# Second attention, blocks of 256 keys: VectorE writes only the negated maximum, ScalarE exponentiates straight from the score bank

## Chip, cores and metric

The kernel runs on one core of one Trainium2 chip. The metric is device microseconds of one execution. TensorE (PE) multiplies, VectorE (DVE), ScalarE (ACT) and GpSimd (POOL) work on its results, SyncE (SP) issues most transfers. PSUM is the accumulator that PE writes and that DVE and ACT read.

## What is computed

Two gated layers over 8 sequences of 256 tokens, width 128. Layer 1 is a recurrence beside a two-deep local-attention network; layer 2 is the attention that this change touches, gated by a mixture of 16 experts (two per token). The part that matters:

```python
def _L1_attn_ref(x, Wq, Wk, Wv, Wo, bo):      # B 2 (here 8 sequences), S 256, 16 heads of 8
    q = (x @ Wq.T).reshape(b, s, H, DK).transpose(0, 2, 1, 3)
    ...
    scores = jnp.einsum('bhqd,bhkd->bhqk', q, k)
    scores = jnp.where(causal, scores, -jnp.inf)
    attn = jax.nn.softmax(scores / np.sqrt(DK), axis=-1)
    ctx = jnp.einsum('bhqk,bhkd->bhqd', attn, v)
    ...
    return ctx @ Wo.T + bo
```

## The kernel before

The 16 token tiles are handled in four turns of four tiles. The program is a chain of sections: HEAD, FIRST (turn 0), BODY (a loop that runs twice), TAIL, LAST, and then the experts. The second attention of a turn runs in the section after it, so it stands in BODY (twice), TAIL and LAST. A planner (`section_order`) writes the order of items for each engine from a table of costs, `PARTS`, and engines work strictly in that order; the items of the other network are interleaved with it.

For each sequence `b` (0, 1) of a turn the second attention has three blocks `q`. Block 0 is the first 128 queries against 128 keys, four heads to a bank; blocks 1 and 2 are the last 128 queries against all 256 keys, two heads to a bank. A block has two pairs `h` of two units; a unit is one PSUM bank of 128x512 scores. The items of a pair are written here as in the planner:

- `bS b q h` on PE (`score_rows`): two mask matmuls, one into each of the two score banks `psS0`, `psS1`, then the scores. The next `bS` or `S` (a pair of the first attention, `scores`) writes the same two banks.
- `bS b q h` on DVE (`less_maxima_of_pair`, L1420 and L1426): per unit a maximum for each head into `MX`, then scores less maximum into the SBUF buffer `PR` (four units deep). The subtraction releases the bank (`s_free`).
- `bE b q r` on ACT (`exponentials`): one Exp of 128x512 in place in `PR`, then `exp_done`.
- `bT b q r` on PE turns the probabilities into the banks `psT`, ACT copies them out (`keep_probs`); `bP` sums with the values, `bN` on DVE normalises.

So PE waits for DVE alone before it writes the score banks again, and ACT may take the Exp much later. Around the change stand these items too: `wo` and `sh` (output product and token shift of the first attention), `w1`, `w2` (its feed-forward part; Gelu on ACT), `qk`, `scale` (DVE and POOL work on queries and keys), `x` (a turn of the activations), `w13`, `w2t` (in LAST: turning expert weights).

Of the kernel before, what the change touches and what calls it, by code (L numbers as in the profile page):

```python
# [18 lines left out]
ALU = mybir.AluOpType  # L19
ACT = mybir.ActivationFunctionType  # L20
AX = mybir.AxisListType.X

P = 128
# [381 lines left out]
class Section:  # L405
# [25 lines left out]
    def turned_before(self, n):  # L431

        return [self.T[unit_item("T", u)] for u in self.S if self.S[u] == n] or self.earlier("T")

    def earlier(self, name):

        n = self.before.get(name, 0)
        return [n - 2, n - 1]
# [38 lines left out]
WIDE = 2 * FE + 2 * D  # L477

T_A0 = T_P_USES // 2
D_FIRST_STEPS, D_A_STEPS, P_A_STEPS = 48, 76, 24  # L480


D_HEAD_STEPS, P_HEAD_STEPS = 1, 5
# [2 lines left out]
def gated_layers(nc, ins, out):  # L486
    ctx = ExitStack()
    with ctx:
# [6 lines left out]
        def pair(name):  # L495
# [3 lines left out]
        Tb, Mb, Sb, Ob = ([ctx.enter_context(nc.psum_tensor(f"ps{n}{i}", [P, 512], F32)) for i in range(2)]  # L499
                          for n in "TMSO")  # L500
        t_full, t_free = pair("t_full"), pair("t_free")
        m_full, m_free = pair("m_full"), pair("m_free")
        s_full, s_free = pair("s_full"), pair("s_free")
        o_free = pair("o_free")
        exp_done = pair("exp_done")
# [25 lines left out]
        PR = sb("PR", [P, 4, 512])  # L531
        PT = sb("PT", [P, 2, 512])
        MX = sb("MX", [P, 4, 4])
# [305 lines left out]
        def _(pe):  # L839
# [12 lines left out]
                    pe.wait_ge(m_free.sem(e), m_free.did(hm, e))  # L852
                return Mb[n % 2]

            def scores(b, qt, hs, n):


                for i in range(2):
                    pe.wait_ge(s_free.sem(n + i), s_free.reuse(hs, n + i))
                    pe.sem_inc(pe_settled, 1)  # L860
                    r = slice(64 * i, 64 * i + 64)
                    for w in range(2):
                        nc.tensor.matmul(Sb[i][64 * w:64 * w + 64, :], identb[r, r],
                                         ((mask0[0], mask1)[qt] if w == i else swapped[qt])[r, :], start=True, stop=False,
                                         skip_group_check=True)
                for c in range(4):
                    for w in range(2):
                        for i in range(2):
                            r = slice(64 * i, 64 * i + 64)
                            q = b * SEQ + qt * P + 64 * w  # L870
                            keys = own_keys(2 * qt + w, r, c, b)
                            o = Sb[i][64 * w:64 * w + 64, c * P:(c + 1) * P]
                            if 2 * qt + w == 2:
                                o = o.rearrange("p (w k) -> p w k", w=2)
                            last = nc.tensor.matmul(o, QT[r, c, q:q + 64], keys, start=False, stop=c == 3,  # L875
                                                    skip_group_check=True)
                            if c == 3 and w == 1:
                                last.then_inc(s_full.sem(n + i), 1)
# [17 lines left out]
                    last = mm(bank[64:P, o], p[:, 64:P], VA[:, 2 * b + qt, head, :])  # L896
                last.then_inc(pv_done.sem(o_use), 1)

            def score_rows(b, q, h, hs, n):


                qt, keys = int(q > 0), P * (1 + (q > 0))
                for i in range(2):
                    pe.wait_ge(s_free.sem(n + i), s_free.reuse(hs, n + i))
                    nc.tensor.matmul(Sb[i][:].rearrange("p (i k) -> p i k", k=keys)[:, :, qt * P:keys], identb[:],
                                     mask0[1][:, 0:512 // (qt + 1)].rearrange("p (i k) -> p i k", k=P),
                                     start=True, stop=False, skip_group_check=True)
                for c, lane in enumerate((range(4), (0, 1), (2, 3))[q]):
                    for i in range(2):
                        r = slice(NS * (2 * h + i), NS * (2 * h + i) + NS)  # L910
                        last = nc.tensor.matmul(Sb[i][:, c * keys:(c + 1) * keys], QL[r, b, lane, qt * P:(qt + 1) * P],  # L911
                                                KT1[r, b * SEQ:b * SEQ + keys], start=False,
                                                stop=(c + 1) * keys == 512, skip_group_check=True)
                        if (c + 1) * keys == 512:
                            last.then_inc(s_full.sem(n + i), 1)
# [30 lines left out]
            def run(sec, it, ahead):  # L946
                ht, hm = T_A0 + uses_before(sec, it, "T"), uses_before(sec, it, "M")
                hs, hq, ho = uses_before(sec, it, "S"), uses_before(sec, it, "QK"), uses_before(sec, it, "O")
# [6 lines left out]
                for item in sec.order["PE"]:  # L955
                    kind, *of = item
                    if kind == "x":
                        l, b = of
# [5 lines left out]
                        for t in range(2):  # L964
                            last = nc.tensor.transpose(bank[:, t * P:(t + 1) * P], XC[:, 2 * b + t, :], ident[:])  # L965
                        last.then_inc(t_full.sem(sec.T[item]), 1)
                    if kind == "ab":
                        copied(("x", 0, 1), earlier=True)
                        bank = m_open(hm, sec.M[item])
                        for i in range(2):  # L970
                            for b in range(2):
                                last = mm(bank[NS * b:NS * b + NS, i * SEQ:(i + 1) * SEQ], WABC[:, i, :],
                                          XNT[:, b * SEQ:(b + 1) * SEQ])
                        last.then_inc(m_full.sem(sec.M[item]), 1)
                    if kind == "c":
                        bank = m_open(hm, sec.M[item])
                        for b in range(2):
                            last = mm(bank[NS * b:NS * b + NS, 0:SEQ], WABC[:, 2, :], XNT[:, b * SEQ:(b + 1) * SEQ])
                        last.then_inc(m_full.sem(sec.M[item]), 1)
                    if kind == "y":  # L980
                        pe.wait_ge(cs_done, it + 1)
                        bank = m_open(hm, sec.M[item])
                        for t in range(GT):
                            mm(bank[:, t * P:(t + 1) * P], CS[0:2 * NS, (t % 2) * P:(t % 2 + 1) * P],
                               WYP[0:2 * NS, t // 2, :], True, False)
                            last = mm(bank[:, t * P:(t + 1) * P], XNT[:, t * P:(t + 1) * P], WD, False, True)
                        last.then_inc(m_full.sem(sec.M[item]), 1)
                    if kind in ("qk", "v"):
                        l, n = of
# [7 lines left out]
                    if kind == "qkT":  # L997
                        l, n = of
# [7 lines left out]
                    if kind == "S":  # L1006
                        l, b, qt = of
                        if sec is FIRST:
                            pe.wait_ge(ld_masks, 16 * 4)
                        if sec is FIRST and (l, b, qt) == (0, 0, 0):  # L1010
                            pe.wait_ge(pool_consts, POOL_CONSTS)
                        if qt == 0:
                            if (l, b) == (0, 0):
                                copied(earlier=True)
                            else:
                                copied(("qkT", l, 4 * b + 2), ("qkT", l, 4 * b + 3))
                        scores(b, qt, hs, sec.S[l, b, 2 * qt])
                    if kind == "T":
                        turn_probs(ht, sec.T[item], hs, sec.S[*of])
                    if kind == "V":  # L1020
# [4 lines left out]
                    if kind == "oT":  # L1025
                        l, t = of
# [80 lines left out]
                    if kind == "bS":  # L1107
                        b, q, h = of
                        if q == h == 0:
                            pe.wait_ge(q_masked, it * 8 + 4 * b)  # L1110
                        score_rows(b, q, h, hs, sec.S["b", b, q, 2 * h])
                    if kind == "bT":
                        turn_probs(ht, sec.T[item], hs, sec.S["b", *of])
                    if kind == "bP":
# [91 lines left out]
        def _(act):  # L1206
# [6 lines left out]
            def exponentials(hs, n):  # L1213
                act.wait_ge(s_free.sem(n), s_free.did(hs, n))
                act_fn(PR[:, n % 4, :], PR[:, n % 4, :], ACT.Exp).then_inc(exp_done.sem(n), 1)
# [12 lines left out]
            def run(sec, it, ahead):  # L1228
# [13 lines left out]
                for item in sec.order["ACT"]:  # L1242
# [77 lines left out]
                    if kind == "bqk":  # L1320
# [3 lines left out]
                        act.wait_ge(q_masked, it * 8 + (4 * b - 4))  # L1324
                        act_fn(QRAW[:], bank[:, 0:SEQ], ACT.Copy, scale=DK1 ** -0.5)
                        act_fn(KT1[:, b * SEQ:(b + 1) * SEQ], bank[:, SEQ:2 * SEQ], ACT.Copy).then_inc(free, 1)
                    if kind == "bE":
                        exponentials(hs, sec.S["b", *of])
                    if kind == "bT":
                        b, q, r = of  # L1330
                        n = B_UNITS * b + 4 * q + r
                        before = sec.earlier("O") if n < 8 else [sec.O["bP", (n - 8) // B_UNITS, int((n - 8) % B_UNITS > 3)]]
                        keep_probs(ht, sec.T[item], ho, before, PTB[:, n % 8, :])
# [61 lines left out]
        def _(dve):  # L1395
# [17 lines left out]
            def less_maxima_of_pair(hs, n, turned, ht, ns):  # L1413

                before = steps[1]
                scores = [Sb[i][:].rearrange("p (s k) -> p s k", s=ns) for i in range(2)]
                maxima = [MX[:, (n + i) % 4, 0:ns] for i in range(2)]
                for i in range(2):
                    dve.wait_ge(s_full.sem(n + i), s_full.did(hs, n + i))
                    V.tensor_reduce(maxima[i], scores[i], AX, ALU.max).then_inc(dstep, 1)  # L1420
                    steps[1] += 1
                for i in range(2):
                    dve.wait_ge(dstep, steps[0] + before + i + 1)
                    for u in turned[i]:
                        dve.wait_ge(t_full.sem(u), t_full.did(ht, u))
                    V.tensor_tensor(PR[:, (n + i) % 4, :].rearrange("p (s k) -> p s k", s=ns), scores[i],  # L1426
                                    maxima[i].unsqueeze(2).broadcast_to([P, ns, 512 // ns]), ALU.subtract)\
                        .then_inc(s_free.sem(n + i), 1)
# [40 lines left out]
            def run(sec, it, ahead):  # L1469
# [22 lines left out]
                for item in sec.order["DVE"]:  # L1492
# [133 lines left out]
                    if kind == "bS":  # L1626
                        b, q, h = of
                        n = sec.S["b", b, q, 2 * h]
                        less_maxima_of_pair(hs, n, [sec.turned_before(n + i - 4) for i in range(2)], ht, 2 if q else 4)
                    if kind == "bN":  # L1630
                        b, qt = of
                        o = sec.O["bP", b, qt]
# [371 lines left out]
```

## Time and profile before

| | us |
|---|---|
| median of 3 runs | 886.46 (882.73 to 886.53) |
| span of the profiled execution | 918.4 |
| BODY, its second pass, about | 174 |
| VectorE busy | 642.1 |
| ScalarE busy | 496.9 |
| PE busy (matmuls) | 708.3 |

The profile is of one execution; its own time, first to last instruction, is the span of 918.4 us, and no other time of that execution is given. It lies 31.9 us above the median of the timed runs. Busy time is the time an engine had an instruction at work; where it waited, the views name the engine and line whose end released it.

### The profile page before, as it was taken

To read this page: it belongs to the slowest core of one execution; us is meant where nothing else is said; L and a number is where in the kernel's file an instruction comes from. 1 tells how busy PE (TensorE), PEld (TensorE's weight loads), DVE (VectorE), ACT (ScalarE), POOL (GpSimd) and SP (SyncE) were. 2 spreads that over 40 slices of the span, in tenths; PEclk is the share of its full clock that TensorE was granted. 3 is DMA by queue.
4 is the path that set the end of the run, shared out by engine and by line. 5 is a ranking of instruction groups with operands and counts; after the bars stand their busy time and mean duration, and the time that the engine had idled before them with its cause. 6 is when DMAs were issued, how large, how long until landed. Compare 5 with 4: busy or idle time off the path is not lost.

```text
span 918.4 us, 20712 instructions
## 1 busy us (share of the span) xinstructions
PE 708.3 (77%) x7336; PEld 530.8 (58%) x7351; DVE 642.1 (70%) x1521; ACT 496.9 (54%) x893; POOL 392.0 (43%) x470
## 2 busy tenths in 40 slices
PE   4688887689899867998997798999859309798830
PEld 1456554457676734676675466658646207698830
DVE  5586776697869775977986797787658325476645
ACT  2444555465666753656676566655726205487711
POOL 7351633560714063434412760480041750068880
PEclk9789999899999997999999999999978759799975
DMA  8600000000000000000000000000023313122104
GB/s 206 177 1 1 1 1 1 1 1 3 1 2 1 2 1 3 2 1 2 1 2 1 1 1 2 1 2 2 1 87 87 119 42 128 36 70 70 62 35 146
DMA packets 43839, 30.03 MB, mean 33 GB/s; under 512 B 7650, under 2 KB 41692, under 8 KB 43484
## 3 DMA queue, kind: packets, MB, share of 16 engines
q1 hardware_dynamic: 39932, 23.17, 8.7%
q0 software_dynamic: 2560, 5.25, 1.5%
q8 instruction: 64, 1.05, 0.5%
q10 hardware_dynamic: 1248, 0.28, 0.2%
q14 instruction: 35, 0.29, 0.1%
HBM read 18.98 MB, written 9.44 MB: 31 GB/s over the span
## 4 chain that ended last, share of the span: by engine, by line
PE 38%; DVE 24%; issue 13%; POOL 13%; ACT 6%; another core or an unknown queue 4%; DMA 1%; DVEq 1%; POOLq 0%; ACTq 0%; SPq 0%
PE psM L841 14%; DVE arena L1538 5%; PE psO L926 4%; ACT arena L1208 4%; DVE PR L1426 4%; PE psT L884 4%; POOL yt_scratch L1918 3%; PE psS L875 3%; PE psS L911 3%; POOL arena L1895 3%; POOL arena L1892 3%; POOL RS L1871 2%; DVE MX L1420 2%; DVE arena L1546 2%
## 5 line engine op out<-in xcount | busy, mean ns | idle before, releaser
L841 PE MATMUL psM<-arena 128*128 128x128 f32 (+7 forms) x1168 | 267.9, 372 | 44.1 <-DVE arena L1538 25.3
L1208 ACT ACTIVATE arena<-psT 128x512 f32<-128x512 f32 (+2 forms) x296 | 150.8, 530 | 153.9 <-PE psT L1003 37.1
L841 PEld LDWEIGHTS psM<-arena 128*128 128x128 f32 (+5 forms) x1168 | 155.5, 190 | 93.0 <-DVE arena L1538 38.1
L1208 ACT ACTIVATE arena<-psM 128x512 f32<-128x512 f32 (+2 forms) x168 | 88.3, 543 | 114.3 <-PE psM L841 113.3
L1420 DVE TENSOR_REDUCE MX<-psS 128x4 f32<-128x512 f32 (+1 forms) x160 | 102.7, 682 | 62.5 <-issue 24.0
L1870 POOL TENSOR_SCALAR RS<-MV 128x2 f32<-128x2 f32 x56 | 14.4, 256 | 293.2 <-DVE MV L1574 167.5
L1892 POOL TENSOR_TENSOR arena<-arena,powm 128x8 f32<-128x8 f32 x64 | 109.9, 1717 | 5.3
L1208 ACT ACTIVATE PR<-PR 128x512 f32<-128x512 f32 x160 | 94.6, 626 | 21.1 <-DVE PR L1426 20.9
L1426 DVE TENSOR_TENSOR PR<-psS,MX 128x512 f32<-128x512 f32 x160 | 102.1, 678 | 0.0
L884 PE MATMUL psT<-ident,PR 128*128 128x128 f32 x640 | 94.3, 282 | 5.4 <-ACT PR L1208 1.9
L884 PEld LDWEIGHTS psT<-ident,PR 128*128 128x128 f32 x640 | 74.9, 145 | 34.1 <-issue 27.0
L1895 POOL TENSOR_TENSOR arena<-arena 128x512 f32<-128x512 f32 x64 | 85.7, 1339 | 0.0
L1538 DVE TENSOR_TENSOR arena<-psM,arena 128x512 f32<-128x512 f32 x128 | 81.7, 679 | 0.0
L1208 ACT ACTIVATE arena<-arena 128x768 f32 (+3 forms) x61 | 46.6, 763 | 49.9 <-DVE arena L1806 30.0
L1546 DVE TENSOR_TENSOR arena<-arena 128x512 f32<-128x512 f32 x64 | 55.1, 878 | 15.3 <-POOL arena L1895 15.2
L1891 POOL TENSOR_SCALAR arena<-arena 128x8 f32<-128x8 f32 x64 | 17.9, 280 | 104.6 <-DVE arena L1525 104.3
L1208 ACT ACT_TABLE_LOAD x43 | 55.2, 1283 | 10.0 <-PE psT L965 9.3
L1525 DVE TENSOR_REDUCE arena<-arena 128x8 f32<-128x512 f32 x64 | 43.4, 678 | 21.0 <-ACT arena L1208 20.6
L1003 PE MATMUL psT<-ident,arena 128*128 128x128 f32 x256 | 40.8, 287 | 19.9 <-DVE arena L1546 19.8
L911 PE MATMUL psS<-arena 32*128 32x256 f32 (+1 forms) x512 | 55.7, 346 | 0.0
L1918 POOL DMA_INDIRECT yt_scratch<-arena,DEST x48 | 49.7, 1036 | 12.1 <-issue 7.3
L1906 POOL TENSOR_SCALAR arena<-arena,lanem 128x256 f32<-128x256 f32 x32 | 29.2, 934 | 55.8 <-ACT arena L1208 55.8
(198 smaller groups left out, 1163.8 us busy)
## 6 DMA issues: line engine op xcount, KB each, us to landing
arena<-in_L_ffn_w SPq DMA_DIRECT2D x50, 128.0 KB
xg_scratch<-zeros SPq DMA_DIRECT2D x12, 256.0 KB, 3.7
arena<-xg_scratch SPq DMA_DIRECT2D x12, 256.0 KB
arena<-yt_scratch SPq DMA_DIRECT2D x4, 512.0 KB, 5.3
arena<-in_L_ffn_wqkv SPq DMA_DIRECT2D x2, 768.0 KB, 5.0
arena<-in_L_ffn_ln_g SPq DMA_DIRECT2D x1, 1024.0 KB, 5.3
arena<-in_L_ffn_ln_b SPq DMA_DIRECT2D x1, 1024.0 KB, 8.5
out<-arena SPq DMA_DIRECT2D x4, 256.0 KB, 2.2
```

What stands on the lines that cost most here:

```text
L841: return nc.tensor.matmul(o, lhsT, rhs, start=start, stop=stop)
L884: last = nc.tensor.transpose(bank[:, c * P:(c + 1) * P], PR[:, m % 4, c * P:(c + 1) * P], ident[:])
L911: last = nc.tensor.matmul(Sb[i][:, c * keys:(c + 1) * keys], QL[r, b, lane, qt * P:(qt + 1) * P], KT1[r, b * SEQ:b * SEQ + keys], start=False,
L1208: return nc.scalar.activation(o, i, f, **kw)
L1420: V.tensor_reduce(maxima[i], scores[i], AX, ALU.max).then_inc(dstep, 1)
L1426: V.tensor_tensor(PR[:, (n + i) % 4, :].rearrange("p (s k) -> p s k", s=ns), scores[i], maxima[i].unsqueeze(2).broadcast_to([P, ns, 512 // ...
L1525: V.tensor_reduce(SS[:, m % 4, :], SQ[:, m % 2, :].rearrange("p (h d) -> p h d", h=8), AX, ALU.add).then_inc(ss_done.sem(m), 1)
L1538: last = V.tensor_tensor(dst.rearrange("p (h d) -> p h d", h=8), src, RT[:, 2 * l + n % 2, x, t % 2, :].unsqueeze(1) .broadcast_to([P, 8, ...
L1546: V.tensor_tensor(r1, r1, RN[:, m % 4, :].unsqueeze(2).broadcast_to([P, 8, DH]), ALU.mult)\
L1892: G.tensor_tensor(RN[:, m % 4, :], RN[:, m % 4, :], powm[:, 0:8], ALU.pow)
L1895: G.tensor_tensor(r1, r1, r2[:, :, ::-1, :], ALU.add).then_inc(rope_sum.sem(m), 1)
L1918: G.indirect_dma_start(YT, bass.IndirectOffsetOnAxis(DEST[:, tile:tile + 1], 0), YO[:, tile % OUT_RING, :], None)\
```

## The change

For the blocks with 256 keys (`q` 1 and 2) DVE no longer subtracts: it takes the maximum with the sign turned and releases its claim on the bank. ACT reads the bank itself: two Exp of 128x256 a unit, with the head's negated maximum as the bias. PE, before it writes a bank whose last unit was of this kind, now also waits for that unit's `exp_done`. The constant 76 counted DVE steps of a BODY and becomes 60. The planner's costs stay, so no item moves.

```diff
+    def read_by_exponent(self, n):
+
+        unit = next((u for u in self.S if self.S[u] == n), None)
+        return unit is None or (unit[0] == "b" and unit[2] > 0)
...
-D_FIRST_STEPS, D_A_STEPS, P_A_STEPS = 48, 76, 24
+D_FIRST_STEPS, D_A_STEPS, P_A_STEPS = 48, 60, 24
...
-            def scores(b, qt, hs, n):
+            def scores(sec, b, qt, hs, n):
...
                 for i in range(2):
                     pe.wait_ge(s_free.sem(n + i), s_free.reuse(hs, n + i))
+                    if sec.read_by_exponent(n + i - 2):
+                        pe.wait_ge(exp_done.sem(n + i), exp_done.reuse(hs, n + i))
...
-                    if kind == "bE":
+                    if kind == "bE" and of[1] == 0:
                         exponentials(hs, sec.S["b", *of])
+                    if kind == "bE" and of[1]:
+                        n = sec.S["b", *of]
+                        act.wait_ge(s_free.sem(n), s_free.did(hs, n))
+                        for u in sec.turned_before(n - 4):
+                            act.wait_ge(t_full.sem(u), t_full.did(ht, u))
+                        for i in range(2):
+                            keys = slice(i * 2 * P, (i + 1) * 2 * P)
+                            last = act_fn(PR[:, n % 4, keys], Sb[n % 2][:, keys], ACT.Exp, bias=MX[:, n % 4, i:i + 1])
+                        last.then_inc(exp_done.sem(n), 1)
...
-                        less_maxima_of_pair(hs, n, [sec.turned_before(n + i - 4) for i in range(2)], ht, 2 if q else 4)
+                        if q == 0:
+                            less_maxima_of_pair(hs, n, [sec.turned_before(n + i - 4) for i in range(2)], ht, 4)
+                        for i in range(2 if q else 0):
+                            dve.wait_ge(s_full.sem(n + i), s_full.did(hs, n + i))
+                            V.tensor_reduce(MX[:, (n + i) % 4, 0:2], Sb[i][:].rearrange("p (s k) -> p s k", s=2),
+                                            AX, ALU.max, negate=True).then_inc(s_free.sem(n + i), 1)
```

The same two waits are added in `score_rows`. How it stands on the engines, in BODY, at the pair `bS 0 1 1` and the pair after it, `bS 0 2 0`:

On DVE, behind the last Gelu product of `w1 0 0 2`, `bS 0 1 1` was this (L1420 the maxima, L1426 the subtractions, L1595 and L1598 the item `w2 0 0`):

```order
L1588 SCALAR_TENSOR_TENSOR arena<-psM,arena 85x256
L1419 REGISTER_ALU
L1420 TENSOR_REDUCE MX<-psS 128x2 x2
L1425 REGISTER_ALU
L1426 TENSOR_TENSOR PR<-psS,MX 128x512
L1423 REGISTER_ALU
L1425 REGISTER_ALU
L1426 TENSOR_TENSOR PR<-psS,MX 128x512
L1478 REGISTER_ALU
L1595 TENSOR_TENSOR arena<-arena,psM 128x256
```

Now it is this:

```order
L1606 SCALAR_TENSOR_TENSOR arena<-psM,arena 85x256
L1650 REGISTER_ALU
L1651 TENSOR_REDUCE MX<-psS 128x2 x2
L1496 REGISTER_ALU
L1613 TENSOR_TENSOR arena<-arena,psM 128x256
```

The two subtractions are gone and `w2` follows the maxima at once. On ACT, the Exp of that pair (`bE 0 1 2`, `bE 0 1 3`) stood behind two copies of `oT` and a table load:

```order
L1208 ACTIVATE arena<-psT 128x512
L1208 ACTIVATE arena<-psM 128x512
L1208 ACTIVATE arena<-psT 128x512
L1214 REGISTER_ALU
L1208 ACT_TABLE_LOAD
L1208 ACTIVATE PR<-PR 128x512 x2
L1239 REGISTER_ALU
```

They stand at the same place now, four in number, and read the bank:

```order
L1217 ACTIVATE arena<-psT 128x512
L1217 ACTIVATE arena<-psM 128x512
L1217 ACTIVATE arena<-psT 128x512
L1340 REGISTER_ALU
L1217 ACT_TABLE_LOAD
L1217 ACTIVATE PR<-psS,MX 128x256 x4
L1248 REGISTER_ALU
```

Nothing moved in the order; the source and the number of the Exp changed. On PE, `bS 0 2 0` follows the turn `oT 0 1` and stands ahead of `wo 0 1`, `qk 1 2` and the turns of the probabilities of `bS 0 1 1` (in brackets the semaphores that an instruction waits for):

```order
L1032 MATMUL psT<-ident,arena 128x128 [waits t_free1,o_free0]
L1032 MATMUL psT<-ident,arena 128x128 x3
L904 REGISTER_ALU
L905 MATMUL psS<-maskc,identb 128x2x128 [waits s_free0]
L905 MATMUL psS<-maskc,identb 128x2x128 [waits s_free1]
L911 MATMUL psS<-arena 128x256 x4
L953 REGISTER_ALU
L852 REGISTER_ALU [waits t_free1,t_free0]
L841 MATMUL psM<-arena 128x128 [waits m_free0]
```

Now the same rows wait for the Exp of the pair before as well:

```order
L1041 MATMUL psT<-ident,arena 128x128 [waits t_free1,o_free0]
L1041 MATMUL psT<-ident,arena 128x128 x3
L911 REGISTER_ALU
L914 MATMUL psS<-maskc,identb 128x2x128 [waits exp_done0,s_free0]
L914 MATMUL psS<-maskc,identb 128x2x128 [waits exp_done1,s_free1]
L920 MATMUL psS<-arena 128x256 x4
L962 REGISTER_ALU
L857 REGISTER_ALU [waits t_free1,t_free0]
L846 MATMUL psM<-arena 128x128 [waits m_free0]
```

Only the waits changed; everything behind the mask matmuls on PE is behind those waits.

## Rows read from the trace of the kernel before

**Rows 1.** The page: its span, and the chain that ended last, by engine and line

```profile
span 918.4 us, 20712 instructions
...
PE 38%; DVE 24%; issue 13%; POOL 13%; ACT 6%; another core or an unknown queue 4%; DMA 1%; DVEq 1%; POOLq 0%; ACTq 0%; SPq 0%
PE psM L841 14%; DVE arena L1538 5%; PE psO L926 4%; ACT arena L1208 4%; DVE PR L1426 4%; PE psT L884 4%; POOL yt_scratch L1918 3%; PE psS L875 3%; PE psS L911 3%; POOL arena L1895 3%; POOL arena L1892 3%; POOL RS L1871 2%; DVE MX L1420 2%; DVE arena L1546 2%
```

**Rows 2.** Busy time by engine, second BODY (stretch; length, PE, PEld, DVE, ACT, POOL)

```profile
346.00:520.00 174.00, 147.75 (x1650) 107.36 (x1650) 135.65 (x288) 106.17 (x184) 68.41 (x74) 0.97 0.01 2
```

**Rows 3.** Groups by line and form: count, busy us, mean ns, idle before

```profile
L1426 DVE TENSOR_TENSOR PR<-psS,MX 128x512 f32<-128x512 f32 x160 | 102.1, 678 | 0.0
L1420 DVE TENSOR_REDUCE MX<-psS 128x2 f32<-128x512 f32 x64 | 41.0, 682 | 10.2 <-PE psS L911 10.1
L1208 ACT ACTIVATE PR<-PR 128x512 f32<-128x512 f32 x160 | 94.6, 626 | 21.1 <-DVE PR L1426 20.9
L1208 ACT ACTIVATE arena<-psM,arena 128x256 f32<-128x256 f32 x32 | 14.4, 473 | 9.2 <-PE psM L841 9.0
```

**Rows 4.** Timeline, BODY, around `bS 0 1 0` and `S 0 1 0`: start, length

```profile
385.51 1.27 PE L875 MATMUL psS<-arena 64*64 64x128 f32 x32
385.89 1.15 ACT L1208 ACTIVATE PR<-PR 128x512 f32<-128x512 f32 x2
387.74 1.95 PE L926 MATMUL psO<-arena 128*32 128x128 f32 x64
389.63 0.40 PE L863 MATMUL psS<-maskl,identb 64*64 64x512 bf16 x1
```

**Rows 5.** Timeline, BODY, from `bS 0 1 1` on: start, length, idle before

```profile
402.40 1.28 DVE L1426 TENSOR_TENSOR PR<-psS,MX 128x512 f32<-128x512 f32 x2
404.52 0.44 PE L965 MATMUL psT<-ident,arena 128*128 128x128 f32 x2 [0.52 <-DVE arena L1598]
409.44 0.38 PE L905 MATMUL psS<-maskc,identb 128*128 128x256 bf16 x2
410.30 1.28 ACT L1208 ACT_TABLE_LOAD   x1
410.81 2.91 PE L841 MATMUL psM<-arena 128*128 128x128 f32 x18
411.60 1.15 ACT L1208 ACTIVATE PR<-PR 128x512 f32<-128x512 f32 x2
414.29 0.41 DVE L1561 TENSOR_TENSOR arena<-arena,psM 128x256 f32<-128x256 f32 x1
427.47 0.69 DVE L1546 TENSOR_TENSOR arena<-arena 128x512 f32<-128x512 f32 x1 [2.26 <-POOL arena L1895]
```

**Rows 6.** Timeline, TAIL, behind `bS 0 1 1` and behind `bS 0 2 1`

```profile
568.87 0.84 ACT L1208 ACTIVATE arena<-psM,arena 128x256 f32<-128x256 f32 x2
570.18 0.28 PE L905 MATMUL psS<-maskc,identb 128*128 128x256 bf16 x1 [1.98 <-DVE PR L1426]
571.02 1.15 ACT L1208 ACTIVATE PR<-PR 128x512 f32<-128x512 f32 x2
575.76 0.42 DVE L1561 TENSOR_TENSOR arena<-arena,psM 128x256 f32<-128x256 f32 x1 [1.13 <-PE psM L841]
...
588.42 0.38 PE L905 MATMUL psS<-maskc,identb 128*128 128x512 bf16 x1
589.02 1.15 ACT L1208 ACTIVATE PR<-PR 128x512 f32<-128x512 f32 x2
```

**Rows 7.** Timeline, LAST: a long wait on ACT, and the last pairs

```profile
755.19 0.60 ACT L1208 ACTIVATE arena<-psT 128x512 f32<-128x512 f32 x1 [32.01 <-remote]
...
779.59 0.27 PE L905 MATMUL psS<-maskc,identb 128*128 128x256 bf16 x1
780.07 1.14 ACT L1208 ACTIVATE PR<-PR 128x512 f32<-128x512 f32 x2
784.65 0.66 PE L884 MATMUL psT<-ident,PR 128*128 128x128 f32 x4 [0.99 <-ACT PR L1208]
```

More of the change, by code:

```diff
@@ L897, in values, with score_rows @@
                 last.then_inc(pv_done.sem(o_use), 1)
-            def score_rows(b, q, h, hs, n):
+            def score_rows(sec, b, q, h, hs, n):
                 qt, keys = int(q > 0), P * (1 + (q > 0))
@@ L904, in score_rows @@
                     pe.wait_ge(s_free.sem(n + i), s_free.reuse(hs, n + i))
+                    if sec.read_by_exponent(n + i - 2):
+                        pe.wait_ge(exp_done.sem(n + i), exp_done.reuse(hs, n + i))
                     nc.tensor.matmul(Sb[i][:].rearrange("p (i k) -> p i k", k=keys)[:, :, qt * P:keys], identb[:],
@@ L1016, in run @@
                                 copied(("qkT", l, 4 * b + 2), ("qkT", l, 4 * b + 3))
-                        scores(b, qt, hs, sec.S[l, b, 2 * qt])
+                        scores(sec, b, qt, hs, sec.S[l, b, 2 * qt])
                     if kind == "T":
@@ L1110, in run @@
                             pe.wait_ge(q_masked, it * 8 + 4 * b)
-                        score_rows(b, q, h, hs, sec.S["b", b, q, 2 * h])
+                        score_rows(sec, b, q, h, hs, sec.S["b", b, q, 2 * h])
                     if kind == "bT":
```

## The prediction

> **What bounds the kernel now.** I read the page's chain first, then the busy times of one BODY, then the timelines around the pairs that change. The chain passes through PE for 38%, DVE for 24%, POOL for 13%, and through no single engine for long [rows 1]. In the second BODY, of 174 us PE is busy 147.75, DVE 135.65, ACT 106.17, POOL 68.41 [rows 2]: PE is the fullest, DVE close behind, ACT has the most room of the engines that change. The chain hops between them, so what a pair is worth is decided at its own place: whoever comes last there. The reader should see that DVE is at times the last (the subtractions L1426 are 4% of the chain), and that ACT, although it is seldom the last, takes some Exp very late: the pair `bS 0 1 1` is subtracted at 402.40 and exponentiated at 411.60 [rows 5]. Before, nobody minded: the score banks were free since the subtraction. That is the state the change touches.
>
> **What is removed.** 64 subtractions at 678 ns (32 pairs: 8 in each BODY, 8 in TAIL, 8 in LAST) leave DVE. Two of them take 1.28 us as a pair, and the next instruction starts about 1.2 us after the first [rows 3, 5], so 38 us of DVE time go in all, 9.6 in a BODY. The maxima stay; I take the negated ones at the old 682 ns [rows 3].
>
> **What is added on ACT.** Two Exp of 128x512 took 1.15 us together, a start every 0.53 [rows 5]. Four of 128x256 with a bias pointer come instead, from PSUM. The trace has that shape as the Gelu of `psM` with a bias: 473 ns alone [rows 3], two in 0.84, so a start every 0.37 [rows 6]. A pair then takes 3 x 0.37 + 0.47 = 1.6 us, 0.45 more; 32 pairs make 14 us on ACT. The first bank is released about 0.85 us after the first Exp starts, the second after 1.6. Bounds: if starts came every 0.30 a pair would take 1.4, if they didn't overlap, 4 x 0.47 = 1.9. [...]
>
> **What is added on PE: a wait.** A `bS` or `S` behind a changed pair now waits until that pair's Exp have read both banks. The first mask matmul waits for the first bank, the second for the second, and the scores stand behind both; behind them stands everything else on PE. Three places show the sizes.
>
> BODY, `bS 0 1 0`: Exp starts at 385.89, behind copies that the change doesn't touch, so the banks are free at 386.75 and 387.5. PE wrote the scores of `S 0 1 0` at 385.51 [rows 4]: 2.0 us later now. Behind them stand turns and a `bP` that kept PE busy right up to 389.63, when the next `S` began; `y` and `w1` follow on a full PE. DVE would have been 1.2 us early there, but has to wait for these scores. I charge 1.9.
>
> BODY, `bS 0 1 1`: PE is ready at 409.44. ACT is at a copy, then the table load at 410.30, then the Exp at 411.60 [rows 5]; none of that depends on DVE, so it stays. The second bank is free at 413.2: PE stands for 3.7 us, with `wo 0 1`, `qk 1 2`, the turns and `sh` behind it. `wo` is 16 of the 18 matmuls of 2.91 us that follow the scores, so its result comes 2 us after them, and DVE's L1561 goes from 414.29 to 416.7, 2.4 late although it had 1.2 us in hand. The next pair's missing subtractions give back 1.2; the rest, 1.2, goes into POOL's chain for `scale`, for which DVE waits at 427.47 [rows 5], and on to PE. Charge 1.2. Ahead of it stands a gain: the turn `x 1 0` at 404.52 waited 0.52 for DVE behind the subtractions of 402.40 [rows 5]: minus 0.5. The later four pairs of a BODY find ACT prompt and either PE or POOL last; I take them at zero, between minus 0.5 and plus 0.5.
>
> One BODY: 1.9 + 1.2 - 0.5 = 2.6, two make 5.2.
>
> TAIL: PE, which wrote at 570.18 after waiting for DVE, gets the banks from Exp that start at 571.02: 571.9 and 572.6. That is 1.9 late, and the path behind it is PE's: DVE waited for `wo` at 575.76. Charge 1.9. At 588.42 PE would have to wait for the Exp of 589.02, so until 590.6, 2.2 late with two `qk` items of the POOL chain behind it: 2.2 [rows 6]. In the second sequence two more waits of this kind, together some 4.5 us on PE, meet a stretch where the missing subtractions give most of it back; I charge 1.2. Together 5.3.
>
> LAST: one wait of 2.2 comes early and puts all that follows back, the routing too. ACT then stands 32.01 us until 755.19 [rows 7] for something that no engine of the program released; a further delay ahead of it may vanish there. Of the last pairs ACT is the busiest engine: PE wrote at 779.59, the Exp ran at 780.07, so the banks come at 781.7 at the best, and PE and ACT, each behind the other twice, end some 3.0 late where PE waits for ACT at 784.65 [rows 7]. Charge 5.2.
>
> **Sum.** 5.2 + 5.3 + 5.2 = 15.7 us. I take off 2 us for places where freed DVE time (38 us) helps that I didn't find: 13.7. Against the profiled execution that is 918.4 to about 932; the timed median lies 31.9 us below that span, near the size of the one long wait on ACT, which may belong to the profiled execution only. I add the difference to the median: 886.5 + 13.7, so about **900 us**, 1.5% slower. A difference of 0.5%, 4.4 us, is about what a measurement of this kernel can tell from none.
>
> **Rivals.**
>
> *DVE's relief wins* (16%): faster. If DVE is last more often than I read, the missing subtractions shorten the chain. L1426 is 4% of the chain, 36 us for 160 of them; 64 of those are 14.7 us. If the waits cost only half of what I charge (7.9), the kernel gains 6.8: 880. At its best, with waits hidden, 872. It decides if PE's 3.7 us in BODY are absorbed before L1561: then each BODY is at least 1 us ahead. For it speaks that DVE is busy 78% of a BODY and that Exp of a prompt pair can start up to 1.2 us earlier; against it, that at the places above ACT's start is fixed by copies and table loads.
>
> *The two cancel* (14%): within 4.4 us of before, 882 to 891, about 888. For it speaks the spread: eleven or so pairs gain, ten lose, and a kernel in which four engines are interleaved absorbs a late microsecond often.
>
> *The waits add up* (9%): nothing is absorbed. Raw PE waits are about 5.9 in a BODY, 8.7 in TAIL, 7 in LAST: 27.5 together, 914. It would need PE to have no idle time behind each wait; it has 26 us in a BODY [rows 2], so I hold this unlikely.
>
> *My forecast* (61%): some of each wait reaches the end; its own range is 892 to 910.
>
> **Range and chances.** Faster 0.16, same 0.14, slower 0.70 (forecast and adding up). The range 882 to 912 leaves out most of the faster case and the end of the adding-up one, about 2 in 10; the price of the Exp (1.4 to 1.9 a pair, over some ten waits plus or minus 3 us) lies within it.
>
> **What would show it.** DVE busy about 43 us less, ACT 14 to 16 more. In BODY, PE idle some 3.7 us ahead of the mask matmul of `bS 0 2 0`, released by ACT's Exp; a BODY of 176.6 instead of 174; PE idle of about 2 us released by ACT at five or so more mask matmuls. Wrong would be: the Exp of `bS 0 1 1` starting earlier than right behind its table load; Exp of 128x256 far from 0.47; a BODY shorter than 174, which would mean that DVE's relief is on the path; or the long wait of LAST moving, which no step here covers.

## The result and the profile after

The changed kernel takes 917.38 us (median of 4, 916.08 to 920.84) against 886.5 (882.73 to 888.35) in the runs beside it, where 900 was forecast and 912 was the upper end. The medians are 3.5% apart; the ratio of the runs is 1.0376 [1.0329, 1.0423] (in brackets, here and below, the 95% interval). One timed run below, the 919.47 of `e8_short_fill`, counts as a slow one and is left out of its ratio. The direction was right; the loss is 31 us instead of 13.7.

The execution profiled of before was an unusual one: its wait of 32.01 us on ACT in LAST [rows 7] is in no other profile here, and its span of 918.4 less this wait gives 886.4, close to the timed median. In the executions of the changed kernel the span is 2 us below the time. So no two spans are subtracted below; the stages are compared, each from its first score mask matmul on PE to that of the next (LAST in two pieces around the long wait: to the mask matmul of its seventh pair, and from the Exp of the eighth to the end of the last pair's Exp):

| us | BODY 1 | BODY 2 | TAIL | LAST, first | LAST, then |
|---|---|---|---|---|---|
| before | 173.4 | 170.0 | 169.7 | 29.7 | 18.0 |
| changed | 177.9 | 177.0 | 175.2 | 36.9 | 23.2 |
| `e1_wait_alone` | 177.7 | 174.1 | 174.7 | 36.2 | 20.4 |
| `e2_relief_alone` | 170.2 | 166.4 | 166.9 | 28.9 | 17.6 |
| `e3_filled_wait` | 177.9 | 176.7 | 175.3 | 36.9 | 23.2 |
| `e5_prompt_pairs` | 172.7 | 169.4 | 170.5 | 29.0 | 18.4 |
| `e6_late_pairs` | 177.3 | 177.3 | 174.7 | 37.0 | 22.8 |
| `e7_one_exp` | 176.6 | 174.5 | 174.8 | 36.2 | 21.8 |
| `e8_short_fill` | 174.5 | 173.0 | 178.5 | 36.7 | 23.2 |
| `e11_body_moved` | 172.4 | 174.8 | 178.8 | 36.7 | 23.2 |
| `e9_moved` | 172.9 | 171.1 | 171.6 | 35.7 | 21.6 |
| `e10_moved_before` | 176.8 | 175.5 | 171.0 | 34.8 | 21.9 |
| `e12_placed` | 170.8 | 169.7 | 169.0 | 29.1 | 18.0 |
| `e13_placed_last_direct` | 172.4 | 171.3 | 169.0 | 36.5 | 21.3 |

The changed kernel loses 4.5 and 7.0 in the BODYs, 5.5 in TAIL, 7.2 and 5.2 in LAST: 29.4. Each row is one execution, and a pass of the same code differs by a microsecond or two from one kernel to the next (the BODYs of the last two rows, by 1.6), which is the grain of this table. The table also shows that a BODY of before is 173.4 or 170.0, not the 174 from which the prediction gave 176.6.

The page of the changed kernel, the chain by engine (answers to [rows 1]):

```profile
PE 42%; DVE 18%; POOL 14%; issue 13%; ACT 11%; DMA 1%; DVEq 1%; POOLq 0%; ACTq 0%; SPq 0%
```

Groups by line and form (to [rows 3]):

```profile
L1217 ACT ACTIVATE PR<-psS,MX 128x256 f32<-128x256 f32 x128 | 50.1, 480 | 3.4 <-DVE MX L1651 3.3
L1651 DVE TENSOR_REDUCE MX<-psS 128x2 f32<-128x512 f32 x64 | 41.1, 683 | 39.5 <-PE psS L920 39.4
```

PE's largest waits (engine, what it waits for: total, times, longest):

```profile
PE psS L914 <- ACT PR L1217: 23.6, 22, 3.8
PE psM L846 <- DVE arena L1556: 21.4, 24, 2.0
```

DVE has become lighter, 601.7 us busy instead of 642.1, and went from 24% of the chain to 18%; ACT went from 6% to 11%. The largest wait of PE is one that did not exist before: the mask matmul behind the Exp. ACT is busy for 508.6 us instead of 496.9, 11.7 more where 14 to 16 were forecast. VectorE now stands 39.4 us ahead of the maxima of these pairs, where it stood 10.1 [rows 3]: the time taken from it came back as waiting for PE.

The place of [rows 5] on PE, `bS 0 2 0` behind `bS 0 1 1`, is where the prediction put its largest wait in BODY:

```profile
417.74 0.37 PE L914 MATMUL psS<-maskc,identb 128*128 128x256 bf16 x1 [2.98 <-ACT PR L1217]
418.47 0.37 PE L914 MATMUL psS<-maskc,identb 128*128 128x256 bf16 x1 [0.35 <-ACT PR L1217]
418.77 2.08 PE L920 MATMUL psS<-arena 32*128 32x256 f32 x8
420.78 4.63 PE L846 MATMUL psM<-arena 128*128 128x128 f32 x18
```

and on ACT and DVE:

```profile
415.46 1.28 ACT L1217 ACT_TABLE_LOAD   x1
416.76 1.56 ACT L1217 ACTIVATE PR<-psS,MX 128x256 f32<-128x256 f32 x4
...
424.59 0.42 DVE L1579 TENSOR_TENSOR arena<-arena,psM 128x256 f32<-128x256 f32 x1 [2.42 <-PE psM L846]
```

The four Exp last 1.56, and the banks come free only behind the table load, as forecast. What was not forecast stands in the last two PE rows: the 18 matmuls of `wo` and `qk` took 2.91 us before [rows 5] and take 4.63 now, and the scores ahead of them go from 1.13 to 2.08. The clock granted to PE says why. Ten microseconds at this place, the scores, `wo` and `qk` in both, before and changed (in the changed kernel the wait takes up the rest); the columns are stretch, us, busy of PE, PEld, DVE, ACT, POOL, then PEclk, DMA share, GB/s:

```profile
411.00:421.00 10.00, 8.92 (x58) 6.17 (x57) 9.85 (x21) 6.62 (x12) 8.34 (x9) 1.00 0.01 2
```

```profile
415.00:425.00 10.00, 6.90 (x28) 5.33 (x29) 3.84 (x8) 3.29 (x6) 5.69 (x5) 0.66 0.00 0
```

A mean of 0.66 is a stretch at half clock (0.50 in 417.7 to 424.3) among full (1.00); the half-clock stretch runs from 417.6 to 424.4 and begins as the wait ends. BODY 1 has the same at 236.7 to 243.5, behind the same wait (0.50 in 236.8 to 243.4). In `e1_wait_alone` and `e7_one_exp` (below) the waits here are 2.77 and 2.83, with 6.8 us at half behind the one in BODY 1 and 3.4 in BODY 2. So half clock follows the wait at both of these places; it does not at every wait: behind one of 3.12 us in TAIL this kernel has full clock (1.00), as shown at `e8_short_fill`.

### The profile page after: what moved, and what is told of

It is laid out like the page before. It is cut to its first block, busy times and chain, and to the rows that moved or that the text cites. A ratio compares the mean times of both kernels' runs of the same rounds, so it can differ in the third digit from the quotient of the medians.

```text
span 914.0 us, 20726 instructions
## 1 busy us (share of the span) xinstructions
PE 722.9 (79%) x7336; PEld 540.6 (59%) x7351; DVE 601.7 (66%) x1457; ACT 508.6 (56%) x957; POOL 392.0 (43%) x470
## 4 chain that ended last, share of the span: by engine, by line
PE 42%; DVE 18%; POOL 14%; issue 13%; ACT 11%; DMA 1%; DVEq 1%; POOLq 0%; ACTq 0%; SPq 0%
PE psM L846 16%; PE psT L891 5%; PE psS L920 5%; ACT arena L1217 4%; PE psO L935 4%; ACT PR L1217 4%; DVE arena L1556 4%; POOL arena L1915 3%; PE psS L882 3%; POOL yt_scratch L1941 3%; POOL arena L1918 3%; POOL RS L1894 3%; ACT L1217 3%; DVE PR L1444 2%; PE psO L846 2%
## 5 line engine op out<-in xcount | busy, mean ns | idle before, releaser
L846 PE MATMUL psM<-arena 128*128 128x128 f32 (+7 forms) x1168 | 272.1, 376 | 39.1 <-DVE arena L1556 21.4
L846 PEld LDWEIGHTS psM<-arena 128*128 128x128 f32 (+5 forms) x1168 | 158.9, 194 | 87.4 <-DVE arena L1556 34.6
L891 PE MATMUL psT<-ident,PR 128*128 128x128 f32 x640 | 97.4, 289 | 4.6 <-ACT arena L1217 2.5
L1438 DVE TENSOR_REDUCE MX<-psS 128x4 f32<-128x512 f32 x96 | 61.6, 683 | 38.7 <-PE psS L882 27.5
L1651 DVE TENSOR_REDUCE MX<-psS 128x2 f32<-128x512 f32 x64 | 41.1, 683 | 39.5 <-PE psS L920 39.4
L1217 ACT ACTIVATE PR<-PR 128x512 f32<-128x512 f32 x96 | 57.1, 626 | 15.2 <-DVE PR L1444 15.1
L920 PE MATMUL psS<-arena 32*128 32x256 f32 (+1 forms) x512 | 61.4, 372 | 0.0
L1444 DVE TENSOR_TENSOR PR<-psS,MX 128x512 f32<-128x512 f32 x96 | 61.3, 679 | 0.0
L1564 DVE TENSOR_TENSOR arena<-arena 128x512 f32<-128x512 f32 x64 | 50.5, 805 | 15.1 <-POOL arena L1918 14.9
L1543 DVE TENSOR_REDUCE arena<-arena 128x8 f32<-128x512 f32 x64 | 43.4, 679 | 23.6 <-ACT arena L1217 23.2
```

The lines of the kernel that those rows point to most:

```text
L846: return nc.tensor.matmul(o, lhsT, rhs, start=start, stop=stop)
L891: last = nc.tensor.transpose(bank[:, c * P:(c + 1) * P], PR[:, m % 4, c * P:(c + 1) * P], ident[:])
L1217: return nc.scalar.activation(o, i, f, **kw)
L1543: V.tensor_reduce(SS[:, m % 4, :], SQ[:, m % 2, :].rearrange("p (h d) -> p h d", h=8), AX, ALU.add).then_inc(ss_done.sem(m), 1)
L1564: V.tensor_tensor(r1, r1, RN[:, m % 4, :].unsqueeze(2).broadcast_to([P, 8, DH]), ALU.mult)\
```

## The experiments

**The wait alone, the relief alone, a filled wait.** Three kernels on one chip (before there: 885.73, 882.17 to 887.72). In the first, the kernel before gets PE's new waits and nothing else:

```diff
                     pe.wait_ge(s_free.sem(n + i), s_free.reuse(hs, n + i))
+                    if sec.read_by_exponent(n + i - 2):
+                        pe.wait_ge(exp_done.sem(n + i), exp_done.reuse(hs, n + i))
```

> The kernel before with one thing added: PE waits for the Exp of a 256-key unit before it writes that unit's bank again. VectorE still subtracts, ScalarE still has one Exp of 128x512 a unit. Theory A (the wait is the cost, the missing subtractions give little back): 912 to 920 us, nearly all of the 31 us. Theory of the relief (the missing subtractions give some 14 us back in the changed kernel): about 930, since here they are not missing. Theory C (the two longer Exp instructions are the cost): 886 to 895.

Measured: 911.38 (910.23 to 914.0), ratio 1.03 [1.0259, 1.034], just under Theory A's range. The wait is worth 25.7 us by itself.

The second is the changed kernel without these waits, with one Exp of 128x512 that reads and writes `PR` as before; the scores of the 256-key pairs do not reach the probabilities:

```diff
-                        for i in range(2):
-                            keys = slice(i * 2 * P, (i + 1) * 2 * P)
-                            last = act_fn(PR[:, n % 4, keys], Sb[n % 2][:, keys], ACT.Exp, bias=MX[:, n % 4, i:i + 1])
-                        last.then_inc(exp_done.sem(n), 1)
+                        act_fn(PR[:, n % 4, :], PR[:, n % 4, :], ACT.Exp, scale=0.1).then_inc(exp_done.sem(n), 1)
```

> The changed kernel without the new wait on PE and with one Exp of 128x512 a unit in place in PR, as before; the maxima and the missing subtractions stay as changed. The scores of 256-key blocks never reach the probabilities (ScalarE works on old contents of PR), so it leaves that part of the computation out. Theory A: the relief of VectorE is worth 0 to 6 us, 880 to 887. Rival (relief on the path): 872 or less.

Measured: 872.44 (870.48 to 873.74), ratio 0.9862 [0.9827, 0.9897]: 13.3 us for the missing subtractions, twice what my theory gave them, and near the 14.7 that the prediction read off the chain for the rival. The two together would give +12.4, and the change costs 31, so the relief is not there in full while PE waits for ACT; how much of it is left `e7_one_exp` shows.

The third puts six spare matmuls of 128x512 into the wait ahead of `bS 0 2 0` in BODY, on the changed kernel:

```diff
+                        if sec is BODY and (b, q, h) == (0, 2, 0):
+                            bank = m_open(hm, sec.M["wo", 0, 1])
+                            for _ in range(6):
+                                mm(bank[:], ident[:], WQKV[:, 0, 0, :])
```

> The changed kernel with six spare 128x512 matmuls of PE (about 3.1 us) ahead of bS 0 2 0 in the two BODY passes, into the bank that wo writes next, so that PE is at work where it waited about 3.0 us for ScalarE. Theory A (only the waiting counts): 917, or up to 2 us more. Theory B (the wait also makes the granted clock fall to half for 6.8 us behind it, and PE's work there takes twice as long): the clock stays at 1.0 there, each BODY is 2 to 4 us shorter, 909 to 913.

Measured: 918.29 (914.58 to 924.49), ratio 1.0398 [1.0348, 1.0449]. That is Theory A's number and not Theory B's, but the filling was too long to tell them apart:

```profile
413.65 5.42 PE L846 MATMUL psM<-arena,ident 128*128 128x512 f32 x12 [0.65 <-DVE arena L1560]
418.90 0.38 PE L914 MATMUL psS<-maskc,identb 128*128 128x256 bf16 x2
```

The mask matmul came behind the spare ones without a wait, 2.3 us after the second bank was free. The scores behind took 1.13 and `wo` and `qk` 2.91, at full clock (1.00 in 411 to 421). `e8_short_fill` has half the filling.

**Which pairs, which instruction, which clock.** Four kernels on one chip (before there: 886.5, 881.27 to 893.06). A table names the pairs that take the new form, and the planner's order stays:

```diff
+    def direct(self, b, q, h):
+
+        return q > 0 and (b, q, h) in DIRECT[self.name]
...
+DIRECT = dict(HEAD=[], FIRST=[],
+              BODY=[(0, 2, 1), (1, 1, 0), (1, 1, 1), (1, 2, 0), (1, 2, 1)],
+              TAIL=[(0, 1, 0), (0, 2, 0), (1, 1, 0), (1, 2, 1)],
+              LAST=[(0, 1, 1), (1, 2, 1)])
```

> Only 16 of the 32 pairs take the new form: those whose next mask matmul found the banks free, or nearly, in the changed kernel (five in each BODY, four in TAIL, two in LAST); the 16 others keep the subtraction. Theory A (the loss sits at the few pairs whose Exp comes late, PE waiting there and running at a lower clock after it): PE hardly waits for ACT at a mask, half of the relief of 13 us is kept, 877 to 884. Theory B (longer Exp and waits cost a little everywhere): half of the change's 31 us stays, 895 to 902.

Measured: 885.23 (881.13 to 889.57, 12 runs), ratio 0.9981 [0.9953, 1.0009]. No loss, as Theory A has it, and no gain either, where it expected 877 to 884: where the Exp is prompt, these 16 pairs together are worth nothing clear of the noise, so their subtractions were off the path.

> The complement: only the 16 pairs whose Exp comes late take the new form. Theory A: nearly the whole loss, 908 to 918, with the 3 us wait at bS 0 2 0 and the granted clock at half behind it. Theory B: half of the loss, 895 to 904.

Measured: 917.86 (914.91 to 926.18), ratio 1.0369 [1.0318, 1.0419]: the whole loss, from half the pairs, and by the table in the same stages. So the cost of the wait sits at the late pairs. The gain of the relief must sit there too, since the prompt ones show none of the 13.3 us; no run took the relief of the late pairs alone.

The price of two instructions, on the changed kernel:

```diff
-                        for i in range(2):
-                            keys = slice(i * 2 * P, (i + 1) * 2 * P)
-                            last = act_fn(PR[:, n % 4, keys], Sb[n % 2][:, keys], ACT.Exp, bias=MX[:, n % 4, i:i + 1])
-                        last.then_inc(exp_done.sem(n), 1)
+                        act_fn(PR[:, n % 4, :], Sb[n % 2][:], ACT.Exp, scale=0.1, bias=lgc[:, 0, 1:2])\
+                            .then_inc(exp_done.sem(n), 1)
```

> One Exp of 128x512 a unit from the score bank, with scale 0.1 and a constant bias column, in place of two of 128x256 with the negated maxima as bias; the maxima are still taken and not used, so the probabilities of the 256-key pairs are others. It prices the two-instruction form. If the waits are what counts and a second instruction only makes each longer by 0.4 us, ten to fifteen times: a pair's Exp last 1.2 us and the kernel takes 908 to 914. Rival: the longer Exp undo the relief (wait alone +25.6, relief alone -13.3, together +12.3 would be 898), so that one Exp gives 896 to 902.

Measured: 908.76 (907.58 to 912.16), ratio 1.0262 [1.022, 1.0304]. The second instruction is worth some 9 us of the 31 (a pair's Exp last 1.26 instead of 1.56); with one Exp the form would still lose 22. The waits alone cost 25.7, so of the 13.3 us of relief some 3 are left beside them. The rival of this run, 896 to 902, is out.

Three spare matmuls in place of six (`range(3)`):

> The changed kernel with three spare 128x512 matmuls instead of six ahead of bS 0 2 0 in BODY, some 2.7 us of work instead of 5.4. If the granted clock behind the wait costs time there: the clock stays full around the wait, PE is back before the banks are free, and the kernel takes 908 to 914, 3 to 9 less than the changed one. Rival (the clock there costs nothing that counts): 915 to 920 as before, with the clock full.

Measured: 915.05 (905.69 to 919.47), ratio 1.0302 [1.0244, 1.036]. Without the longest run it is 914.03. That lies between the 908 to 914 expected and the rival's 915 to 920, so the whole time does not decide; the stages do. Its timeline and window, to be held against those of the changed kernel above:

```profile
412.17 2.84 PE L846 MATMUL psM<-arena,ident 128*128 128x512 f32 x6 [0.65 <-DVE arena L1560]
414.85 0.65 PE L914 MATMUL psS<-maskc,identb 128*128 128x256 bf16 x2
415.43 1.13 PE L920 MATMUL psS<-arena 32*128 32x256 f32 x8
416.50 2.91 PE L846 MATMUL psM<-arena 128*128 128x128 f32 x18
```

```profile
411.00:421.00 10.00, 8.92 (x52) 5.77 (x50) 6.06 (x11) 5.41 (x11) 6.26 (x6) 1.00 0.00 0
```

The scores and `wo` are back at 1.13 and 2.91, the clock at 1.00, with useless work added and the banks coming no sooner (the Exp start 11.14 us after `bS 0 1 1` in both kernels). The BODYs take 174.5 and 173.0 instead of 177.9 and 177.0, 7.4 us less. Of these, 5.6 lie between `bS 0 1 1` and the next sequence's first mask matmul, where the filling is; another 1.5 lie ahead of it in BODY 2, where a stretch at half clock behind `S 0 1 0` (390.3 to 393.7 in the changed kernel, 0.50) is gone though nothing was changed there. The whole kernel shows 2.3 to 3.4, not clear of the spread of its runs. TAIL is 3.4 longer, and the profile has a stretch at half clock there (674.9 to 685.1, 0.50) where the changed kernel had none over the same work, 1.00 in 672 to 692 (first this kernel, then the changed one):

```profile
675.62 2.90 PE L846 MATMUL psM<-arena 128*128 128x128 f32 x12 [3.12 <-DVE arena L1610]
...
681.01 5.68 PE L935 MATMUL psO<-arena 128*32 128x128 f32 x128 [0.78 <-ACT arena L1221]
```

```profile
681.92 1.58 PE L846 MATMUL psM<-arena 128*128 128x128 f32 x12 [3.12 <-DVE arena L1606]
...
685.20 3.70 PE L935 MATMUL psO<-arena 128*32 128x128 f32 x128 [0.83 <-DVE arena L1613]
```

Nothing was changed there, and the wait ahead of this work is 3.12 us in both. So a wait of 3 us on PE can be followed by half clock and need not be; what decides it stays open.

**Moving the work instead of filling.** Three kernels on one chip (before there: 885.55, 881.94 to 889.36). After planning, single items are moved on their engine:

```diff
+    for engine, item, behind in MOVED.get(name, []):
+        order[engine].remove(item)
+        order[engine].insert(order[engine].index(behind) + 1, item)
```

```diff
+    "BODY": [
+        ('PE', ('S', 0, 1, 0), ('bT', 0, 1, 1)),
+        ('PE', ('bS', 0, 2, 0), ('qk', 1, 2)),
+        ('DVE', ('bS', 0, 2, 0), ('wo', 0, 1)),
+    ],
+    "TAIL": [
+        ('PE', ('bS', 0, 2, 0), ('wo', 0, 1)),
+        ('DVE', ('bS', 0, 2, 0), ('wo', 0, 1)),
+        ('PE', ('bS', 1, 0, 0), ('x', 1, 1)),
+        ('DVE', ('bS', 1, 0, 0), ('qk', 1, 1)),
+        ('PE', ('bS', 1, 2, 0), ('sh', 1, 1)),
+        ('DVE', ('bS', 1, 2, 0), ('sh', 1, 1)),
+    ],
+    "LAST": [
+        ('PE', ('bS', 0, 1, 1), ('bT', 0, 1, 1)),
+        ('PE', ('bS', 0, 2, 1), ('bT', 0, 2, 1)),
+        ('PE', ('bS', 1, 1, 1), ('bT', 1, 1, 1)),
+        ('PE', ('bS', 1, 2, 1), ('bT', 1, 2, 1)),
+    ],
```

> The changed kernel with the order of PE (and of VectorE where it follows) altered at eight places, so that work that does not need the Exp stands ahead of a late pair's successor: in BODY S 0 1 0 behind bT 0 1 1 and bS 0 2 0 behind qk 1 2 (VectorE: behind wo 0 1), three such places in TAIL, four in LAST. Theory A (the loss is PE standing, and then at half clock, with other work queued behind the mask matmul): most of the 31 us goes, 886 to 900, and the half-clock stretches behind the waits in BODY go too. Rival C (the pair itself is on the path, since its own result is late, whatever PE does meanwhile): 908 to 918.

Measured: 899.49 (896.9 to 901.42), ratio 1.0158 [1.0128, 1.0189]. Of 31 us, some 17 are gone. The BODYs and TAIL are back within 2 us of before; LAST keeps 9.6 of its 12.4.

> The same moves on the kernel before, as the base for the run above. Its banks are free at the subtraction, so a move can only put a pair later: 886 to 896 by either theory. If it is below 886, the moves are a gain of their own and must be taken off from the other run.

Measured: 904.37 (900.96 to 907.71), ratio 1.0209 [1.0175, 1.0243]. The moves are no gain of their own: they cost the kernel before 19 us, where 10 at most was expected, 9 of them in the BODYs and 9 in LAST by the table. In this order the new form is the faster one, by 4.9 us, though the two intervals still overlap by a little (1.0189 and 1.0175): it costs 31 us in the one order and nothing, or less, in the other. That other order is the slower one for both kernels.

The one move of `bS 0 2 0` in BODY:

> The changed kernel with the one move in BODY alone: bS 0 2 0 behind wo 0 1 and qk 1 2 on PE, behind wo 0 1 on VectorE. Theory A: the two BODYs, which lost 11.7 us together in the changed kernel, lose 4 to 6, so 909 to 913, with the clock full at 237 and at 418 us. Rival C: 915 to 920.

Measured: 911.99 (906.63 to 912.62), ratio 1.0286 [1.0252, 1.0319], as Theory A has it, and BODYs of 172.4 and 174.8. The half-clock stretches at 237 and 418 us are gone; one of 3.4 us at 424.3 (0.50) is new. TAIL is as long as with the short filling, with the same stretch at half clock behind the same wait of 3.12.

**A version from the parts.** Two kernels on one chip (before there: 885.56, 879.19 to 890.44). The table of pairs and the moves together, with what paid:

```diff
+              BODY=[(0, 1, 1), (0, 2, 0), (0, 2, 1), (1, 1, 0), (1, 1, 1), (1, 2, 0), (1, 2, 1)],
+              TAIL=[(0, 1, 0), (0, 1, 1), (0, 2, 0), (0, 2, 1), (1, 1, 0), (1, 2, 0), (1, 2, 1)],
+              LAST=[])
```

> A version meant to beat both. The new form in 21 of the 32 places where a gain was seen or nothing lost: in BODY all pairs but bS 0 1 0, in TAIL all but bS 1 1 1, in LAST none; and the moves that paid: in BODY bS 0 2 0 behind qk 1 2 on PE and behind wo 0 1 on VectorE, in TAIL bS 0 2 0 behind wo 0 1 and bS 1 0 0 behind x 1 1 (VectorE: qk 1 1). Theory A (an exponent reading the bank costs only where PE stands for it): BODY gains 1 to 2 us each, TAIL 1 to 2, so 878 to 884. Rival C: 886 or above, since the moved pairs are later.

Measured: 880.93 (877.41 to 886.47, 12 runs), ratio 0.9953 [0.9927, 0.9979]: half a per cent faster than before and 4% faster than the changed kernel. PE at the place of the long wait:

```profile
407.75 2.91 PE L871 MATMUL psM<-arena 128*128 128x128 f32 x18 [0.92 <-ACT arena L1242]
410.49 0.38 PE L939 MATMUL psS<-maskc,identb 128*128 128x256 bf16 x2
```

`wo` and `qk` now stand where the wait of 2.98 was, and the mask matmul finds its banks free. Which of the pairs and moves bring the gain was not taken apart.

> The same with LAST in the new form for all its eight pairs, without moves there: the difference to the run above is the cost of the change in LAST alone. By the shifts read in the changed kernel's trace (8.3 us ahead of the long wait, 5.2 behind it) 12 to 14 us, so 891 to 897; by the prediction's sum 5.2, 884 to 888.

Measured: 897.31 (893.19 to 901.19), ratio 1.0124 [1.0094, 1.0155], at the upper end of the 891 to 897 that the trace gave, and far from the 884 to 888 of the prediction's sum. The medians differ by 16.4, of which the two pieces of LAST in the table show 10.7 in the profiled executions; another 3.2 stand in the BODYs, whose code is the same. LAST costs 11 to 16 us, not 5.2.

## Why the prediction was wrong

**The places and the waits were right.** The Exp of a pair last 1.56 us, where 1.6 was forecast. PE stands for the Exp ahead of `bS 0 2 0`, right behind the table load, for 3.3 us in two pieces (3.7 forecast), and DVE is 40 us lighter for 43. Over the kernel PE waits 27.3 us for ACT at the mask matmuls (23.6 and 0.7 by name, and twice 1.51 ahead of `S 0 1 0`, which the profile puts down to no engine but which end as the first bank's Exp do); the prediction's raw waits were 27.5. The second sequence of a BODY, with the four later pairs, is worth nothing, as taken: in BODY 2 it takes 87.4 us for 87.6. `e5_prompt_pairs` shows the same for these and for the other eight pairs that it changes. So what failed is how much of each wait reaches the end, and with it the price of the work behind it.

**BODY, 5.2 forecast, 11.5 measured.** From `bS 0 1 0` to `bS 0 1 1` 1.9 was charged; the delay is 1.4 in BODY 1 and 2.9 in BODY 2, where 3.4 us at half clock stand in it. From `bS 0 1 1` to the second sequence 0.7 was charged (1.2 less 0.5), and the two BODYs lose 3.1 and 4.7. The failed step is the sequel of the 3.7 us wait, in the prediction's words "its result comes 2 us after them, and DVE's L1561 goes from 414.29 to 416.7". `bS 0 1 1` starts 5.90 us later in the changed kernel (405.62 for 399.72), so 416.7 corresponds to 422.6; the row above has 424.59. Most of the missing 2.0 is the half clock: 0.95 on the scores and some 1.5 on the `wo` part of the 18 matmuls, less 0.7 by which the Exp came earlier than I had it. I priced a wait of PE by its length and took the work behind it at its old duration. `e8_short_fill` measures the term: with the clock kept full there the BODYs lose 1.1 and 3.0, 4.1 in all, near the 5.2, and from `bS 0 1 1` on 0.2 and 1.9.

**TAIL, 5.3 forecast, 5.5 measured.** The first wait was charged 1.9 and costs 1.8, and the whole first sequence costs 5.4 where 4.1 was charged. That the total fits is in part luck: the kernel before has half clock behind its wait of 2.73 at 664.49 (0.50 in 664.5 to 667.7; 12 matmuls 2.90), and the changed one has full clock behind 3.12 (1.58, above). In `e8_short_fill` and `e11_body_moved`, with the same TAIL, it takes 178.5 and 178.8, so 9 us more than before.

**LAST, 5.2 forecast, 12.4 in the trace and 11 to 16 by `e13_placed_last_direct`.** The failed step is "one wait of 2.2 comes early" and then a hope that the long wait of [rows 7] hides what follows. No other profile has such a wait, and the timed executions leave no room for it. Ahead of it 2.2 was charged and 7.2 is measured, behind it 3.0 and 5.2. And there is not one early wait but several; here those behind `bS 0 1 0` and behind `bS 0 2 1`, changed kernel, PE:

```profile
721.59 0.37 PE L914 MATMUL psS<-maskc,identb 128*128 128x256 bf16 x1 [1.56 <-ACT PR L1217]
...
722.62 2.08 PE L920 MATMUL psS<-arena 32*128 32x256 f32 x8
...
742.39 0.59 PE L914 MATMUL psS<-maskc,identb 128*128 128x512 bf16 x1 [2.02 <-ACT PR L1217]
```

Here too the scores take nearly twice 1.13, at a clock of 0.51 (721.5 to 728.3). From this mask matmul (of `bS 0 1 1`) to the next pair's 8.32 us pass, where 5.12 passed before for the same work; 2.5 of the difference is longer scores (2.08 for 1.13), turns (1.97 for 1.17) and sums with the values (2.74 for 1.96). In LAST the score pairs follow each other closely, and PE waits for an Exp at one after another, which would hand each wait on; that is argued from the order and not tested. How the 11 to 16 us as a whole divide between wait and clock was not measured.

**"I take off 2 us" for relief that I didn't find.** There was relief, 13.3 us of it, more than I credited, but in a kernel without the waits; beside them some 3 are left. The rival had its size right and its condition wrong: it asked whether the wait is absorbed, while the wait falls on the very pairs that the relief helps.

**The rivals.** "The waits add up", 914 at 9%, is the nearest. Its reason against, that PE has 26 us of idle time in a BODY, was no protection: behind the wait of 2.98 us the 18 matmuls took 4.63 us instead of 2.91. That nothing is absorbed is not what happened either: in the BODYs of `e8_short_fill` the banks come as late as in the changed kernel, and 4.1 us of the 12 of raw waits reach the end. With the clock's part the changed kernel is back at 11.5.

## What to carry to other kernels

Moving a read of a shared buffer to an engine that runs late moves the buffer's release too (here PE then stood 2.98 us ahead of `bS 0 2 0`): list, for each use, when the new reader starts and what stands behind the next writer, before counting what the old reader saves. Price a wait on PE as what of it reaches the end plus, as a risk, the slower clock on the work behind it: in BODY that was 2.7 us behind a wait of 3, in TAIL of the changed kernel nothing behind one of 3.1. Independent work put in front of the wait helps if the moved item can spare the delay; the change cost 31 us in one order and nothing in another, but that other order cost 19 by itself. A change can be taken pair by pair: with some late pairs kept as they were and others given work to stand behind, it is worth 0.5%.

## What the chip showed that was not expected

- Behind the wait of 2.98 us in each BODY PE runs at half clock (0.50) for 6.8 us: 8 score matmuls 2.08 instead of 1.13, 18 of `wo` and `qk` 4.63 instead of 2.91. Three useless matmuls in the wait bring both back; the two BODYs are 7.4 us shorter, 5.6 of it at this place.
- The same wait of 3.12 us in TAIL is followed by half clock in one kernel (12 matmuls 2.90) and by full clock in another (1.58), with the same code there.
- The gain doesn't stay whole: with the BODYs shorter, a stretch of 10 us at half clock (0.50, 674.9 to 685.1) stands in TAIL under unchanged work, in `e8_short_fill` and again in `e11_body_moved` (673.5 to 683.7).
- Exp from PSUM with a bias pointer: 128x256 takes 0.48 us, four in a row 1.56; 128x512 takes 0.69 (`e7_one_exp`), against 0.63 in SBUF without a pointer [rows 3].
